# Expert weights of a sandwich kernel: from a resident copy in SBUF to one DRAM load per slot, with the last tiles in slots of their own

## The chip, the cores and the metric

The kernel runs on one core of one Trainium2 chip. The metric is the device time of one execution in microseconds (us); lower is better. The engines are TensorE (PE, with its weight loads as PEld), VectorE (DVE), ScalarE (ACT), GpSimd (POOL) and SyncE (SP), and 16 DMA engines move data.

## What is computed

The input is 16 sequences of 512 tokens with 128 features. Stage one is a state-space block with a convolution and a scan, and a residual. Stage two is a mixture of 16 experts, of which each token uses two:

```python
probs = jax.nn.softmax(xf @ Wr + br, axis=-1)
vals, idx = jax.lax.top_k(probs, K)               # K = 2, E = 16
w = vals / vals.sum(axis=-1, keepdims=True)
...
for ei in range(e):
    h = jax.nn.silu(xf @ W1[ei]) * (xf @ W3[ei])  # 128 -> 512
    y = h @ W2[ei]                                # 512 -> 128
    mu = y.mean(axis=-1, keepdims=True)
    var = ((y - mu) ** 2).mean(axis=-1, keepdims=True)
    y = (y - mu) * jax.lax.rsqrt(var + EPS) * gamma[ei] + beta[ei]
    out = out + combine[:, ei:ei + 1] * y
```

The result gets a layer norm and is added to the tokens that went in.

## The kernel before

Three stages follow one another, all unrolled by Python and put in order by hand, each engine with its own stream.

**Stage one** runs over the 16 sequences (`NS`) as a software pipeline. At its end VectorE picks two experts for each token, ranks the tokens of each expert with a running count (`running`), and GpSimd sends each token's row (128 values, the token's number, its weight; 520 bytes) to its place in the DRAM tensor `slots_scratch` with indirect DMAs (`send_one`, L612). Each expert has a region of its own there.

**Stage two** works through 143 slots (`NSLOT`), a slot being 128 rows of one expert. With 8192 tokens and two experts each there are 16384 rows, and each expert's last tile is not full. So that it holds no stale rows, 128 blank rows are stored behind the end of every region once the counts are known (`store_tail`, L324 to L326; half by SyncE, half by ACT). VectorE works out a table (`slot_table`) with each slot's expert and first row. Four slot columns go through TensorE to one row (the selection matmuls, L2086), and VectorE copies that row (L1536).

For slot j SyncE reads the table and loads the 128 rows to `got`, eight slots ahead (`load_slots`, L490). TensorE transposes them (`x_t`, L2098), ACT copies them to `xsT`. TensorE multiplies by the two up weights (`up`, L2106, 8 passes each for `pA` and `pR`), ACT takes the silu, VectorE multiplies (`hidT`), and TensorE multiplies by the down weights of the slot before (`down`, L2114). VectorE and GpSimd norm and weigh the result (`ers`, `erw`, `yo`), and GpSimd scatters it to `chosen_scratch` (`store`, L698).

The up weights of all 16 experts (8 MB) lie in SBUF in `w13_sb`: SyncE loads four experts (L408, 2 MB) and the other twelve (6 MB) near the end of stage one. ACT copies the 4 KB per partition of the slot's expert to one of four `stage` buffers, two slots ahead (`put_weights`, L1023), from which TensorE reads. The down weights lie in `w2_sb`.

**Stage three** loads both results of each token from `chosen_scratch` to `w13_sb`, adds them on TensorE, norms them and adds `x1`, which lies in `fx1` (one load of 4 MB, L497).

Filler matmuls (`keep_warm`, L1636) stand where TensorE would idle. SyncE's stream is one queue: what stands behind a wait is not issued. The line numbers are those of the kernel before.

## Time and profile before

| | |
|---|---|
| median of 3 runs | 968.43 us (967.34 to 970.10) |
| the profiled execution | 968.34 us, of which 966.5 us are the span |
| granted TensorE clock, mean | 0.99 |
| busy: PE, DVE, ACT, POOL | 97%, 75%, 71%, 64% |
| stage one with the passage to stage two | 0 to 516.6 us |
| expert slots | 516.6 to about 915 us |
| last stage | to 966.5 us |

All times inside the execution are us from the start of its span. A timeline's row gives start, duration, engine, line and operation, output and inputs, count, and in brackets how long the engine was idle before it and what it waited for; "issue" there means that it waited for nothing that the profile shows. A matmul of fp32 shows as two passes. SPq is SyncE's own stream, with the DMAs it issues.

### The profile page before, as it was taken

To read this page: it belongs to the slowest core of one execution; us is meant where nothing else is said; L and a number is where in the kernel's file an instruction comes from. 1 tells how busy PE (TensorE), PEld (TensorE's weight loads), DVE (VectorE), ACT (ScalarE), POOL (GpSimd) and SP (SyncE) were. 2 spreads that over 40 slices of the span, in tenths; PEclk is the share of its full clock that TensorE was granted. 3 is DMA by queue.
4 is the path that set the end of the run, shared out by engine and by line. 5 is a ranking of instruction groups with operands and counts; after the bars stand their busy time and mean duration, and the time that the engine had idled before them with its cause. 6 is when DMAs were issued, how large, how long until landed. Compare 5 with 4: busy or idle time off the path is not lost.

```text
span 966.5 us, 26600 instructions
## 1 busy us (share of the span) xinstructions
PE 933.1 (97%) x7177; PEld 826.0 (85%) x7177; DVE 724.8 (75%) x2524; ACT 688.3 (71%) x1355; POOL 621.8 (64%) x814
## 2 busy tenths in 40 slices
PE   7999999999999999998959999999999999999995
PEld 4777877888878877887949999999999999999962
DVE  2379999999999998898823777677677677777747
ACT  3777787777788787775215778777777777877626
POOL 2445677777777777775661666666666666576647
PEclk9999999999999999999979999999999999999998
DMA  4001322121111111101786211111111111121076
GB/s 137 12 12 34 93 95 84 58 73 54 56 57 50 56 40 42 40 23 42 263 311 192 69 50 49 46 52 51 44 50 50 45 50 47 45 53 49 19 274 248
DMA packets 52255, 75.25 MB, mean 78 GB/s; under 512 B 11103, under 2 KB 30689, under 8 KB 51472
## 3 DMA queue, kind: packets, MB, share of 16 engines
q1 hardware_dynamic: 41632, 54.61, 18.4%
q0 software_dynamic: 8672, 16.93, 5.2%
q10 hardware_dynamic: 1808, 2.02, 0.7%
q8 instruction: 63, 1.03, 0.5%
q14 instruction: 80, 0.66, 0.2%
HBM read 47.09 MB, written 27.41 MB: 77 GB/s over the span
## 4 chain that ended last, share of the span: by engine, by line
PE 79%; DVE 8%; POOL 6%; issue 5%; DMA 1%; ACT 1%; POOLq 0%; DVEq 0%; SPq 0%; ACTq 0%
PE pA L2106 11%; PE pR L2106 11%; PE pA L1665 11%; PE pB L2114 6%; PE pY L2114 5%; PE pY L1779 4%; PE pB L1691 3%; PE pB L1825 3%; PE pA L1680 3%; PE pY L1815 3%; POOL chosen_scratch L698 2%; PE pY L1798 2%; PE pY L1747 2%; PE pA L1636 2%; PE pR L1763 2%
## 5 line engine op out<-in xcount | busy, mean ns | idle before, releaser
L698 POOL DMA_INDIRECT chosen_scratch<-yo,got_id x143 | 148.2, 1036 | 93.7 <-issue 87.9
L1026 ACT ACTIVATE stage<-w_sb 128x1024 f32 x143 | 151.3, 1058 | 56.6 <-issue 56.5
L1545 DVE TENSOR_TENSOR hidT<-pR,sil 128x512 f32<-128x512 f32 x143 | 98.9, 692 | 80.1 <-ACT sil L1021 59.2
L612 POOL DMA_INDIRECT slots_scratch<-xrow,send_at x128 | 134.6, 1052 | 34.1 <-issue 31.2
L2106 PE MATMUL pA<-xsT,stage 128*128 128x128 f32 x1144 | 151.3, 275 | 0.4 <-ACT xsT L1010 0.4
L2106 PE MATMUL pR<-xsT,stage 128*128 128x128 f32 x1144 | 151.1, 275 | 0.0
L2106 PEld LDWEIGHTS pA<-xsT,stage 128*128 128x128 f32 x1144 | 139.2, 192 | 0.7 <-ACT xsT L1010 0.6
L2106 PEld LDWEIGHTS pR<-xsT,stage 128*128 128x128 f32 x1144 | 139.0, 192 | 0.0
L1665 PE MATMUL pA<-xn,taps 128*128 128x512 f32 x256 | 129.8, 593 | 1.0 <-ACT xn L763 1.0
L688 POOL TENSOR_TENSOR ers<-eve,neg_half 128x1 f32<-128x1 f32 x143 | 81.5, 570 | 57.3 <-DVE eve L1557 32.2
L1021 ACT ACTIVATE sil<-pA 128x512 f32<-128x512 f32 x143 | 85.3, 596 | 25.3 <-PE pA L2106 15.3
L564 POOL TENSOR_TENSOR R<-R,dec 128x512 f32<-128x512 f32 x48 | 64.0, 1334 | 40.6 <-ACT Rh L861 40.0
L2114 PE MATMUL pB<-w_sb,hidT 128*128 x576 | 76.2, 275 | 0.0
L2114 PE MATMUL pY<-w_sb,hidT 128*128 x568 | 75.0, 275 | 0.0
L1016 ACT ACTIVATE wb<-gb,got 128x128 f32 x143 | 57.6, 403 | 19.5 <-issue 11.5
L2114 PEld LDWEIGHTS pB<-w_sb,hidT 128*128 128x128 f32 x576 | 70.1, 192 | 0.2 <-issue 0.2
L2114 PEld LDWEIGHTS pY<-w_sb,hidT 128*128 128x128 f32 x568 | 69.1, 192 | 0.0
L1636 PE MATMUL pA<-ident 128*128 128x128 f32 x446 | 57.1, 288 | 0.4 <-issue 0.4
L1636 PEld LDWEIGHTS pA<-ident 128*128 128x128 f32 x446 | 55.3, 204 | 2.0 <-issue 1.8
L1665 PEld LDWEIGHTS pA<-xn,taps 128*128 128x128 f32 x256 | 40.8, 191 | 13.7 <-issue 12.5
L1779 PE MATMUL pY<-G,RT 128*128 128x128 f32 x384 | 50.8, 275 | 0.0
L1570 DVE SCALAR_TENSOR_TENSOR yo<-yg,erw,wb 128x128 f32<-128x128 f32 x143 | 49.1, 343 | 1.6 <-POOL erw L691 1.5
(233 smaller groups left out, 2099.1 us busy)
## 6 DMA issues: line engine op xcount, KB each, us to landing
got<-slots_scratch SPq DMA_DIRECT2D x143, 65.0 KB, 1.8
w_sb<-chosen_scratch SPq DMA_DIRECT2D x16, 512.0 KB, 5.4
w_sb<-in_w_dram SPq DMA_DIRECT2D x1, 6144.0 KB
xin<-in_x_dram SPq DMA_DIRECT2D x16, 256.0 KB
xr<-in_x_dram SPq DMA_DIRECT2D x16, 256.0 KB
x_scratch<-x SPq DMA_DIRECT2D x16, 256.0 KB
w_sb<-in_w_dram SPq DMA_DIRECT2D x4, 1024.0 KB, 8.2
fx<-x_scratch SPq DMA_DIRECT2D x1, 4096.0 KB
```

The lines of the kernel that those rows point to most:

```text
L564: eng.tensor_tensor(halves(R[:, :, :], h)[:, :, 0:h], src, pairs(decs(s, h))[:, :, 1:2].broadcast_to([P, SEQ // h, h]), ALU.mult).then_inc ...
L612: eng.indirect_dma_start(slots_d, bass.IndirectOffsetOnAxis(ap=send_at[:, s % 2, k, t:t + 1], axis=0), xrow[:, s % 2, k, t, :], None).then ...
L688: eng.tensor_tensor(ers[:, q % 2:q % 2 + 1], eve[:, q % 2:q % 2 + 1], neg_half[:, 0:1], ALU.pow).then_inc(epow, 1)
L698: eng.indirect_dma_start(chosen_d, bass.IndirectOffsetOnAxis(ap=got_id[:, j % NGOT:j % NGOT + 1], axis=0), yo[:, q, :], None, bounds_check ...
L1021: eng.activation(sil[:, p, :], pA[:, p, :], ACT.Silu).then_inc(sil_ready, 1)
L1026: eng.activation(stage[:, j % NSTAGE, :, :].rearrange("p k f -> p (k f)"), w13_sb[:, bass.ds(e, 1), :, :].rearrange("p o k f -> p (o k f)" ...
L1545: eng.tensor_tensor(hidT[:, p, :], pR[:, p, :], sil[:, p, :], ALU.mult).then_inc(hid_ready, 1)
L1636: eng.matmul(pA[:, 1, 0:P], w, w, start=True, stop=True)
L1665: i = eng.matmul(pA[:, f, :], taps[:, k, tile(f)], xn[:, s % 2, w], start=k == 0, stop=k == TAPS - 1)
L1779: i = eng.matmul(pY[:, BANK[h], (2 * m + g) * P:(2 * m + g + 1) * P], RT[:, AT[h], g, m, :], G[:, AT[h], g, :], start=True, stop=True)
L2106: i = eng.matmul(out[:, j % 2, tile(c)], stage[:, j % NSTAGE, k, tile(c)], xsT[:, j % 2, :], start=True, stop=True)
L2114: i = eng.matmul((pB, pY)[p][:, 1, 0:D], hidT[:, p, tile(c)], w2_sb[:, c, bass.ds(e, 1), :].rearrange("p o d -> p (o d)"), start=c == 0, s ...
```

## The change

- `w13_sb` is no longer filled with up weights, and ACT's copies are gone. SyncE loads the 512 KB of the slot's expert from DRAM to a `stage` buffer (`load_weights`): it reads the expert from the table, waits until the buffer's last user is through (`h3_mm`), and issues. Each of the four buffers has a semaphore of its own.
- Order on SyncE: `got` of slot 0, weights of slot 0, and so on for four slots, four more `got`; then for each slot the weights (four slots ahead) and, behind a wait for `erw`, `got_id` and `wb` of the slot eight before, the next `got`. The 4 MB of `x1` are loaded in 16 pieces, one at every fourth slot from the 16th to the 76th.
- The table: `running` starts at 128 instead of 0, so rows begin 128 rows into the region. The first 128 rows of every region are blanked at the start (one DMA of 1 MB on SyncE). The full tiles of all experts (a count of (n - 1) // 128 each) take the first 127 slots (`NFULL`). The last 16 slots are one per expert and read the last 128 rows before the expert's end; they may overlap the full tiles or reach into the blank rows. The `store_tail` stores and their semaphores are gone.
- Overlapping rows are stored twice with the same values, and before slot 127's store GpSimd waits until all earlier stores have landed.
- `keep_warm(40)` behind the selection matmuls becomes `keep_warm(22)`. VectorE fills the table's last 16 entries in two further operations. The wait for `gb_loaded` moves to its first use.

```diff
+    NFULL = NSLOT - NE
...
-        def store_tail(eng, e):
-            row = eng.value_load(tail_at[0:1, e:e + 1], min_val=0, max_val=BLANK - P)
-            eng.dma_start(slots_d[bass.ds(row, P), :].rearrange("(p r) d -> p (r d)", r=8), blank[:, :]).then_inc(tails_stored, 16)
...
+            eng.dma_start(slots_d[0:BLANK, :].rearrange("(e r) d -> e r d", e=NE)[:, 0:P, :].rearrange("e (p r) d -> p e (r d)", r=8),
+                          blank[:, :].rearrange("p (o f) -> p o f", o=1).broadcast_to([P // 8, NE, 8 * ROW])).then_inc(blank_stored, 16)
...
-            load_early()
...
-            eng.wait_ge(tail_ready, 1)
-            for e in range(0, NE, 2):
-                store_tail(eng, e)
...
+            def load_weights(j):
+                e = eng.value_load(slot_table[0:1, j:j + 1], min_val=0, max_val=NE - 1)
+                wait_past(eng, h3_mm, j - NSTAGE + 1)
+                eng.dma_start(stage[:, j % NSTAGE, :, :], w13[:, bass.ds(e, 1), :, :].rearrange("p o k f -> p (o k) f")).then_inc(staged[j % NSTAGE], 16)
+
             for j in range(NGOT):
                 load_slots(j)
-            eng.dma_start(fx1[:, :, :, :], x1_d.rearrange("(g p t) d -> p g t d", p=P, t=NT4)).then_inc(fx1_loaded, 16)
-            for n in range(NGOT, NSLOT):
+                if j < NSTAGE:
+                    load_weights(j)
+            for n in range(NGOT, NSLOT + NGOT - NSTAGE):
+                load_weights(n - NGOT + NSTAGE)
+                if n >= NSLOT:
+                    continue
+                if n % 4 == 0 and 4 <= n // 4 < 4 + NG:
+                    g = n // 4 - 4
+                    eng.dma_start(fx1[:, g, :, :], x1_d[g * NT4 * P:(g + 1) * NT4 * P, :].rearrange("(p t) d -> p t d", t=NT4)).then_inc(fx1_loaded, 16)
...
+                if j == NFULL:
+
+                    for k in range(4):
+                        eng.wait_ge(stored[k], len(range(k, NFULL, 4)) * 16)
...
-            put_weights(0)
             xst(0, 0)
-            put_weights(1)
...
-                if j + 2 < NSLOT:
-                    put_weights(j + 2)
...
+                eng.tensor_scalar(running[:, :], running[:, :], float(P), None, ALU.add).then_inc(lower_ready, 1)
...
-            r.step(eng.tensor_scalar(count_i[:, :], count_i[:, :], P - 1, None, ALU.add))
+            r.step(eng.tensor_scalar(count_i[:, :], count_i[:, :], -P - 1, 0, ALU.add, ALU.max))
...
-            eng.tensor_copy(slot_table[:, :], pA[0:1, 0, :]).then_inc(table_ready, 1)
+            r.step(eng.tensor_copy(slot_table[:, :], pA[0:1, 0, :]))
+            eng.tensor_copy(slot_table[0:1, NFULL:NSLOT], iota_es[0:1, :]).then_inc(table_ready, 1)
+            eng.tensor_scalar(slot_table[0:1, TABLE_ROW + NFULL:TABLE_ROW + NSLOT], running[0:1, :], float(-P), None, ALU.add).then_inc(table_ready, 1)
...
-            keep_warm(40)
+            keep_warm(22)
...
-                    eng.wait_ge(staged, j + 1)
+                    eng.wait_ge(staged[j % NSTAGE], j // NSTAGE * 16 + 16)
```

SyncE at the end of stage one, before: the weight loads of 2 and 6 MB, `gamma` and `beta`, then eight tail stores (the last is shown, seven are left out), and the first `got`.

```order
67 L408 DMA w_sb<-in_w_dram 128x12288 [waits y_step]
68 L386 DMA gb<-in_gamma_dram 128x2048
69 L386 DMA gb<-in_beta_dram 128x2048
70 L373 DMA x_scratch<-x 128x512 [waits x1_ready]
...
99 L325 TENSOR_LOAD tail_at
100 L325 ISA x2
101 L326 ISA
102 L326 DMA slots_scratch<-blank 16x1040
103 L492 TENSOR_LOAD slot_table [waits x1_stored,blank_stored,tails_stored,sent0,stage1_dve,sent1,stage1_pool,table_ready,stage1_act,stage1_pe]
104 L492 ISA x2
105 L493 ISA
106 L493 DMA got<-slots_scratch 128x130
```

The same place now. TENSOR_LOAD is the read of the table, the ISA rows belong to it.

```order
67 L373 DMA gb<-in_gamma_dram 128x2048 [waits y_step]
68 L373 DMA gb<-in_beta_dram 128x2048
69 L368 DMA x_scratch<-x 128x512 [waits x1_ready]
70 L457 TENSOR_LOAD slot_table [waits x1_stored,blank_stored,sent0,stage1_dve,sent1,stage1_pool,table_ready,stage1_act,stage1_pe]
71 L457 ISA x2
72 L458 ISA
73 L458 DMA got<-slots_scratch 128x130
74 L461 TENSOR_LOAD slot_table
75 L461 ISA x2
76 L463 ISA
77 L463 DMA stage<-in_w_dram 128x1024
```

The two weight loads and the tail stores are gone, and slot 0's weights stand right behind slot 0's `got`.

SyncE at the start of the loop, before: the x1 load (`fx`), then a `got` load per slot, each behind its wait.

```order
135 L497 DMA fx<-x_scratch 128x16x512
136 L492 TENSOR_LOAD slot_table [waits wb_ready,id_ready,erw_ready]
137 L492 ISA x2
138 L493 ISA
139 L493 DMA got<-slots_scratch 128x130
140 L492 TENSOR_LOAD slot_table [waits wb_ready,id_ready,erw_ready]
141 L492 ISA x2
142 L493 ISA
143 L493 DMA got<-slots_scratch 128x130
```

Now, behind the first eight `got` loads:

```order
118 L461 TENSOR_LOAD slot_table
119 L461 ISA x2
120 L463 ISA [waits h3_mm]
121 L463 DMA stage<-in_w_dram 128x1024
122 L457 TENSOR_LOAD slot_table [waits wb_ready,id_ready,erw_ready]
123 L457 ISA x2
124 L458 ISA
125 L458 DMA got<-slots_scratch 128x130
126 L461 TENSOR_LOAD slot_table
127 L461 ISA x2
128 L463 ISA [waits h3_mm]
129 L463 DMA stage<-in_w_dram 128x1024
```

Each slot has two table reads and two DMAs; the weights of slot 5 stand behind the `got` that waits for `erw` of slot 0.

ACT in one slot of the loop, before:

```order
685 L1021 ACTIVATE sil<-pA 128x512 [waits h1_mm]
686 L1010 ACTIVATE xsT<-pB 128x128 [waits h3_mm,xs_t]
687 L1013 TENSOR_LOAD slot_table
688 L1013 ISA x2
689 L1016 ISA [waits got_loaded1]
690 L1016 ACTIVATE wb<-gb,got 128x128
691 L1024 TENSOR_LOAD slot_table
692 L1024 ISA x2
693 L1026 ISA
694 L1026 ACTIVATE stage<-w_sb 128x1024
```

Now:

```order
647 L999 ACTIVATE sil<-pA 128x512 [waits hid_ready,h1_mm]
648 L986 ACTIVATE xsT<-pB 128x128 [waits h3_mm,xs_t]
649 L989 TENSOR_LOAD slot_table
650 L989 ISA x2
651 L994 ISA [waits got_loaded2]
652 L994 ACTIVATE wb<-gb,got 128x128
```

The table read and the 128 x 1024 copy are gone.

GpSimd's store of slot 127 now, among its neighbours (before, it waited for `yo_ready` and `id_ready` alone):

```order
677 L678 DMA chosen_scratch<-yo,got_id 16384x128 [waits yo_ready,id_ready]
678 L664 TENSOR_TENSOR ers<-eve,neg_half 128x1 [waits evar_ready]
679 L667 TENSOR_TENSOR erw<-ers,got 128x1 [waits yo_ready,epow]
680 L678 DMA chosen_scratch<-yo,got_id 16384x128 [waits stored2,stored1,stored3,stored0,yo_ready,id_ready]
681 L664 TENSOR_TENSOR ers<-eve,neg_half 128x1 [waits evar_ready]
682 L667 TENSOR_TENSOR erw<-ers,got 128x1 [waits yo_ready,epow]
683 L678 DMA chosen_scratch<-yo,got_id 16384x128 [waits yo_ready,id_ready]
```

Behind that store stand the power and `erw` of slot 129.

## Rows read from the trace of the kernel before

The columns of rows 2 are: the stretch and its length, then for PE, PEld, DVE, ACT and POOL the busy us with the number of instructions, the granted clock, the mean busy share of the DMA engines, and GB/s. Rows 10 has the same.

**Rows 1.** shares of the page: busy us, share of the span, instructions

```profile
PE 933.1 (97%) x7177; PEld 826.0 (85%) x7177; DVE 724.8 (75%) x2524; ACT 688.3 (71%) x1355; POOL 621.8 (64%) x814
```

**Rows 2.** table of stretches: busy us per engine, clock, DMA share, GB/s

```profile
499.00:504.60 5.60, 1.49 (x4) 0.53 (x5) 0.00 (x0) 0.00 (x0) 2.95 (x4) 0.54 0.81 215
504.60:509.60 5.00, 4.93 (x24) 4.92 (x24) 0.68 (x1) 0.00 (x0) 0.00 (x0) 0.50 0.54 80
509.60:516.00 6.40, 6.40 (x59) 6.40 (x58) 0.00 (x0) 1.06 (x1) 0.00 (x0) 0.99 0.17 42
530.00:900.00 370.00, 370.00 (x3318) 370.00 (x3318) 260.70 (x930) 294.61 (x531) 238.84 (x399) 1.00 0.19 51
```

**Rows 3.** timeline of TensorE: start us, busy us, what, [idle before]

```profile
489.69 5.66 PE L1636 MATMUL pA<-ident 128*128 128x128 f32 x36
495.33 0.27 PE L2086 MATMUL pA<-ident,slot_cols 128*1 128x128 f32 x1
...
503.92 0.37 PE L2086 MATMUL pA<-ident,slot_cols 128*1 128x128 f32 x1 [1.76 <-issue]
504.67 11.47 PE L1636 MATMUL pA<-ident 128*128 128x128 f32 x80 [0.37 <-issue]
515.98 0.27 PE L2098 MATMUL pB<-ident,got 128*128 128x128 f32 x1
516.62 1.16 PE L2106 MATMUL pA<-xsT,stage 128*128 128x128 f32 x8 [0.37 <-ACT xsT L1010]
...
524.37 1.06 PE L2106 MATMUL pA<-xsT,stage 128*128 128x128 f32 x8
...
527.15 1.06 PE L2106 MATMUL pA<-xsT,stage 128*128 128x128 f32 x8
```

**Rows 4.** groups by line: count, busy us, mean ns, idle before

```profile
L1026 ACT ACTIVATE stage<-w_sb 128x1024 f32 x143 | 151.3, 1058 | 56.6 <-issue 56.5
```

**Rows 5.** timeline of SyncE's DMA issues, 494 to 530

```profile
494.53 13.92 SPq L326 DMA_DIRECT2D slots_scratch<-blank  x7
511.01 8.11 SPq L493 DMA_DIRECT2D got<-slots_scratch  x8
```

**Rows 6.** waits of SyncE, 480 to 530: us in total, times, longest

```profile
SPq L485 <- DMA slots_scratch<-blank: 1.5, 1, 1.5
```

**Rows 7.** timeline of GpSimd, 500 to 525

```profile
501.90 0.96 POOL L612 DMA_INDIRECT slots_scratch<-xrow,send_at  x1 [0.30 <-issue]
```

**Rows 8.** DMA view, 560 to 900: queues, issues, us to landing

```profile
q8 instruction: 28, 0.46, 0.6%
...
got<-slots_scratch SPq DMA_DIRECT2D x122, 65.0 KB, 1.8
chosen_scratch<-yo,got_id POOLq DMA_INDIRECT x122, 2.3
```

**Rows 9.** line L510, the 512 KB loads of the last stage

```profile
L510 SPq DMA_DIRECT2D w_sb<-chosen_scratch x16: 359/360/471, 923.4 to 943.0; - x16
...
DMA to landing us min/median/max: 3.8/5.4/7.4
```

**Rows 10.** table of stretches, in the 2 MB weight load

```profile
464.00:468.00 4.00, 3.28 (x29) 2.90 (x27) 3.86 (x7) 2.88 (x6) 3.08 (x4) 1.00 1.03 383
```

**Rows 11.** timeline of VectorE, 495 to 525

```profile
505.03 0.68 DVE L1536 CAST slot_table<-pA 1x512 int32<-1x512 f32 x1 [10.05 <-PE pA L2086]
```

**Rows 12.** timeline of one slot in the loop, 699.5 to 706

```profile
699.98 3.13 SPq L493 DMA_DIRECT2D got<-slots_scratch  x2
...
700.08 1.06 PE L2106 MATMUL pA<-xsT,stage 128*128 128x128 f32 x8
...
701.83 0.19 POOL L691 TENSOR_TENSOR erw<-ers,got 128x1 f32<-128x1 f32 x1
```

**Rows 13.** DMA view, 516 to 530: issues with median us to landing

```profile
chosen_scratch<-yo,got_id POOLq DMA_INDIRECT x2, 5.6
```

**Rows 14.** chain of waits at the loop's end

```profile
921.20 2.11 DMA chosen_scratch<-yo,got_id
```

More of the change, by code:

```diff
@@ L101, in sandwich @@
     chosen_d = nc.dram_tensor("chosen_scratch", [2 * NTOKENS, D], fp32).ap()
-    assert NSLOT <= 2 * P and BLANK + P < NOWHERE
+    assert NSLOT <= 2 * P and NFULL >= (2 * NTOKENS - 1) // P and BLANK + P < NOWHERE
     ctx = ExitStack()
@@ L322, in sandwich @@
         sum_bank = lambda g: w13_sb[:, 0, 0, :] if g == 0 else (pA, pB, pR, pY)[g % 8 // 2][:, g % 2, :]
-        def store_tail(eng, e):
-            row = eng.value_load(tail_at[0:1, e:e + 1], min_val=0, max_val=BLANK - P)
-            eng.dma_start(slots_d[bass.ds(row, P), :].rearrange("(p r) d -> p (r d)", r=8), blank[:, :]).then_inc(tails_stored, 16)
         blank_ready, blank_stored, e_loaded = sem("blank_ready"), sem("blank_stored"), sem("e_loaded")
         pool_passed, dve_passed = sem("pool_passed"), sem("dve_passed")
-        w13_loaded = sem("w13_loaded")
-        staged = sem("staged")
+        staged = [sem(f"staged{q}") for q in range(NSTAGE)]
         w2_loaded = sem("w2_loaded")
@@ L339, in sandwich @@
         stage1_sp = sem("stage1_sp")
-        tables, tail_ready, tails_stored = sem("tables"), sem("tail_ready"), sem("tails_stored")
+        tables = sem("tables")
         cols_ready, cols_mm, table_ready = sem("cols_ready"), sem("cols_mm"), sem("table_ready")
@@ L482, in _ @@
                 eng.wait_ge(q, 1)
-            eng.wait_ge(tails_stored, 16 * NE)
-            eng.wait_ge(blank_stored, 16)
+            eng.wait_ge(blank_stored, 32)
             for p in range(2):
                 eng.wait_ge(sent[p], NS // 2 * 2 * NT4 * 16)
-            eng.wait_ge(table_ready, 1)
+            eng.wait_ge(table_ready, 2)
             def load_slots(j):
@@ L997, in _ @@
             eng.nop().then_inc(stage1_act, 1)
-            eng.wait_ge(tail_ready, 1)
-            for e in range(1, NE, 2):
-                store_tail(eng, e)
             for q in (stage1_pe, stage1_dve, stage1_pool, stage1_sp):
                 eng.wait_ge(q, 1)
-            eng.wait_ge(gb_loaded, 32)
-            eng.wait_ge(table_ready, 1)
+            eng.wait_ge(table_ready, 2)
             def xst(j, p):
@@ L1013, in weighed_beta @@
                 e = eng.value_load(slot_table[0:1, j:j + 1], min_val=0, max_val=NE - 1)
+                if not j:
+                    eng.wait_ge(gb_loaded, 32)
                 wait_past(eng, yo_ready, j - 3)
@@ L1021, in silu @@
                 eng.activation(sil[:, p, :], pA[:, p, :], ACT.Silu).then_inc(sil_ready, 1)
-            def put_weights(j):
-                e = eng.value_load(slot_table[0:1, j:j + 1], min_val=0, max_val=NE - 1)
-                wait_past(eng, h3_mm, j - NSTAGE + 1)
-                eng.activation(stage[:, j % NSTAGE, :, :].rearrange("p k f -> p (k f)"), w13_sb[:, bass.ds(e, 1), :, :].rearrange("p o k f -> p (o k f)"), ACT.Copy).then_inc(staged, 1)
-            eng.wait_ge(w13_loaded, 32)
-            put_weights(0)
             xst(0, 0)
-            put_weights(1)
             for j in range(NSLOT):
@@ L1550, in normalise @@
                 e = eng.value_load(slot_table[0:1, j:j + 1], min_val=0, max_val=NE - 1)
+                if not j:
+                    eng.wait_ge(gb_loaded, 32)
                 eng.wait_ge(yo_mm, j + 1)
```

36 lines of the change are left out of this document (4 added, 32 removed).

## The prediction

> **What bounds the kernel now.** I read three views in this order. First the page's shares: TensorE is busy for 97% of the span [rows 1]. That figure hides two things, the filler matmuls (L1636) and the clock, so next comes the table of stretches. From 530 to 900 us, the expert loop, TensorE is busy for the whole 370 us at full clock, with the DMA engines at 0.19 [rows 2]. One slot takes 2.79 us there (527.15 less 524.37 at the start of the loop, [rows 3]). Nothing but TensorE sets the pace, and ACT, which copies the weights of every slot (143 copies of 1058 ns, 151.3 us, [rows 4]), only fills its own idle time. **Taking the copies off ACT is therefore worth nothing in the loop by itself.** The time can move in the passage between the stages. The last real work of stage one on TensorE ends near 489.7, the first matmul of an expert starts at 516.62 [rows 3], and the chain of waits between them is filler, eight gaps of "issue" and 80 more filler passes. The eight selection passes of L2086 take 9 us (495.33 to 504.3) where their own time is 0.27 to 0.37 each, and the filler behind them runs to 515.98 [rows 3]. In the same stretch SyncE stores seven blank tails for 13.92 us, waits 1.5 us for them to land, and issues the first load of `got` only at 511.01 [rows 5, 6].
>
> **The change, part by part.**
>
> *Tails.* The sixteen stores of `blank` at known row counts go, and with them the wait for `tails_stored`. What is late next for SyncE is the end of the sends. GpSimd issues the last one at 501.90 [rows 7]; a store of the same kind lands 2.3 us after its issue [rows 8], so at 504.2. From the wait for the tails (508.45 + 1.5 = 509.95, and about 0.1 more) to the first `got` issue at 511.01 were 0.96 us. With 0.3 us for the semaphores between GpSimd and SyncE (an estimate) the first `got` is issued at 504.2 + 0.3 + 0.96 = 505.5, where it was 511.01.
>
> *First weights.* They no longer lie in SBUF. SyncE issues `got` and weights in turn, and one such issue with its table read costs (8.11 - 0.34)/7 = 1.11 us [rows 5]. Slot 0's weights go out at 506.6. The trace has no load of 512 KB of 4 KB pieces, so I bound its landing. Below stands the `got` load, 65 KB in 1.8 us [rows 8]; above stands the 512 KB load of the last stage, 5.4 us in the median with a least of 3.8, several of them queued behind one another [rows 9]. The fixed part of the first plus the data at the rate that the DMA engines show at full share (524 KB at 383 GB/s, 1.4 us, [rows 10]) is 3.2 us. I take that, since in the loop the DMA engines are at 0.19 and the load queues behind nothing. Slot 0 can start at 509.8.
>
> *Filler and clock.* `keep_warm` goes from 40 to 22 calls, 80 to 44 passes. If the selection passes lose their gaps (the 6 MB weight load, the tail stores and the table reads of SyncE and ACT that ran beside them are gone) the filler is over near 502 (44 passes at 6.40/59 = 0.108 us, [rows 2]), and TensorE idles for some 7 us. In the trace TensorE was sparse from 495.3, the clock stood at half (0.54) from 499, and it was full again only at 509.6, 5.0 us after the filler had resumed [rows 2]. The same after 509.8 costs 2.5 us. Slot 4 starts 10.53 us after slot 0 [rows 3], so at 509.8 + 10.5 + 2.5 = 522.8, where it was 527.15: **4.3 us gained**. If the gaps stay, the selection ends at 504.3, the filler at 511.8 (24 passes in the 5.0 us at half clock, 20 at 0.108), the table is copied by 505.71 [rows 11], two small DVE operations of some 0.2 us follow, and with the 0.96 of above the first `got` goes out near 507.1. Slot 4's weights are the thirteenth issue: 507.1 + 12 x 1.11 = 520.4, and land at 523.6: 3.5 us gained. In the first case the thirteenth issue lands at 518.8 + 3.2 = 522.0, just in time. I take 4.2.
>
> *The loop.* Each slot now adds a table read and a 512 KB load on SyncE. The load for slot j+5 stands behind the `got` load that waits for `erw` of slot j. From the steady part [rows 12]: slot j+2 starts at 700.08, `erw` of slot j starts at 701.83, and the `got` issue follows 0.94 later (699.98 is behind the `erw` one slot of 2.79 us earlier, 699.04). The weights go out 1.11 later, at 703.88, which is 3.80 after slot j+2 began. Slot j+5 starts 3 x 2.79 = 8.37 after it. **The load has 4.57 us to land**, against the 3.2 taken. SyncE itself works 2 x 1.11 us of 2.79, and 0.43 us more in the 16 slots that carry a piece of the x1 load. The DMA engines get 1.4 us of 2.79 on top of 0.19, in all 0.69. One instruction packet holds an engine for about 1.2 us (28 packets, 0.6% of 16 engines over 340 us, [rows 8]): 3.2 + 1.2 = 4.4 is still inside, but with little left, and where two such things meet TensorE waits a few tenths. I put **0.5 us** on the loop (an estimate; bounds 0 and the rival below).
>
> *Last tiles in slots of their own.* The number of slots stays 143. At slot 127 GpSimd waits until all earlier stores have landed. Behind the waiting store stand the power and `erw` of slot 129, and behind these SyncE. The store before it went out 2.79 us earlier and lands after 2.3 [rows 8], so the wait is over when it is reached; with the 5.6 us of the busiest stretch [rows 13] it would be 2.8 us once. The blank slots now lie inside the first 127, so the very last store is a real one: it lands in 2.3 instead of 2.11 us [rows 14], **0.2 us lost**.
>
> *At nothing.* The blank store of 1 MB at the start (SyncE, covered by stage one, where TensorE runs without it), one DVE operation on 16 columns, the x1 load in 16 pieces (it was one 4 MB load beside slots that kept their pace), `gb_loaded` waited for later.
>
> Sum against the profiled execution: 968.34 - 4.2 + 0.2 + 0.5 = 964.8. The median of the runs is 0.09 above it, which gives **964.9**.
>
> **The rivals.**
>
> *The weights come late in the loop.* The point from which it decides is a mean landing of 4.57 us. Every 0.1 us beyond it lengthens a cycle of five slots by 0.1, so the loop by 0.1 x 139/5 = 2.8 us. At 4.9 us, between 4.4 and the 5.4 of the last stage, 0.33 gives 9.2 us: 964.4 + 9.2 = 974. At 5.4 it would be 987. For it: the least 512 KB load took 3.8, not 3.2, and the margin is one instruction packet. Against it: the 5.4 belongs to a queue of such loads, and here each is alone.
>
> *The passage gives nothing.* The stall ends later than I think and the clock stays low longer. With 5.4 us for the first weights slot 0 starts at 512.0; with the clock at half for 10 us, as in the trace from 499 to 509.6, it loses 5 us: slot 4 at 527.5, no gain, 969. Against it: both have to go wrong together.
>
> *The pitch of the rows in DRAM.* Each partition's 4 KB lie 64 KB apart. If reads at that pitch ran at half rate, a slot's load would hold the DMA engines for 2.7 us, and with 0.19 x 2.79 = 0.5 they would need 3.2 us a slot: 0.4 x 143 = 59 us more, 1022. The row speaks against it: the 2 MB load of four experts at the same pitch ran at 383 GB/s [rows 10], though in pieces of 16 KB. The Trainium skill ("DMA: Bandwidth & Descriptors", "Latency and other measured facts") says that row pitches at large powers of two in HBM cost rate, and lists a large loss from 2 MiB on and next to none at 512 KiB. By its figures this pitch would be harmless, and the trace agrees as far as it goes.
>
> *It does better.* Without loss of clock and with 1.8 us of landing, slot 4 would start when its weights are there, 518.8 + 1.8 = 520.6: 6.5 us gained, 962.
>
> **How the numbers follow.** The forecast case gets 0.60 (964.9, its own range 962.0 to 966.5), late weights 0.20, the empty passage 0.15, the pitch 0.05. A measurement of this kernel can tell about 0.3%, 2.9 us: faster is below 965.5. Faster gets 0.54 (0.06 of the forecast case lies nearer), the same 0.22 (0.06, 0.12 of the empty passage, 0.04 of weights that are only a little late), slower 0.24 (0.16, 0.03, 0.05). The range goes from the best case, 962.0, to 975.0; outside it lie the pitch, the heavy half of the late weights, and 0.04 below.
>
> **What would show it.** In the profile of the changed kernel: the first `got` near 505.5, the first weights in `stage` some 4.3 us behind it, selection passes without gaps, the first expert matmul near 510 at half clock, slot 4 near 523; in the loop TensorE full at 2.79 us a slot, landings near 3.2 us, DMA near 0.7, no wait of L2106's up matmuls for a load. Wrong would be landings over 4.5 us, waits of TensorE for `stage` in the loop, GpSimd standing at slot 127 for more than 1 us, or an expert loop that is not full.

## The result, and the profile after

| | before | after |
|---|---|---|
| median | 968.01 us (967.34 to 970.10, 4 runs) | 975.37 us (974.31 to 975.98, 4 runs) |
| ratio | | 1.0066, interval 1.0045 to 1.0087 |
| span of the profiled execution | 966.5 us | 974.1 us |
| granted TensorE clock, mean | 0.99 | 0.991 |

The forecast was 964.9 us with a range from 962.0 to 975.0. The change makes the kernel slower by 0.66%, where the forecast had it 0.4% faster. The page of after, shares and queues:

```profile
PE 934.8 (96%) x7141; PEld 824.9 (85%) x7141; DVE 724.4 (74%) x2526; ACT 538.1 (55%) x1212; POOL 621.2 (64%) x814
...
q1 hardware_dynamic: 62192, 121.74, 42.3%
...
q8 instruction: 63, 1.03, 0.5%
...
HBM read 113.67 MB, written 27.41 MB: 145 GB/s over the span
```

TensorE's busy time is that of [rows 1], plus 1.7 us, in a span that is 7.6 us longer. It is kept from work, and not slowed in it. SyncE's queue (q1) fills 42% of the 16 DMA engines (18.4% before): 143 loads of 0.52 MB stand in the place of 8.4 MB, most of the 113.67 MB read. q8 is the 63 instruction packets of 16 KB that are spoken of below; a further 80 instruction packets of 8 KB go over q14. TensorE's timeline shows the passage between the stages (start us, busy us, what, idle before and its releaser):

```profile
494.38 1.03 PE L2055 MATMUL pA<-ident,slot_cols 128*1 128x128 f32 x8
496.42 0.73 PE L1605 MATMUL pA<-ident 128*128 128x128 f32 x5 [1.01 <-issue]
...
502.15 4.86 PE L1605 MATMUL pA<-ident 128*128 128x128 f32 x26 [0.42 <-issue]
...
510.66 1.13 PE L2075 MATMUL pA<-xsT,stage 128*128 128x128 f32 x8 [2.73 <-DMA stage<-in_w_dram]
...
513.09 1.13 PE L2075 MATMUL pA<-xsT,stage 128*128 128x128 f32 x8 [0.29 <-DMA stage<-in_w_dram]
...
522.76 1.13 PE L2075 MATMUL pA<-xsT,stage 128*128 128x128 f32 x8 [1.07 <-issue]
```

and SyncE's first issues stand there so:

```profile
505.70 0.36 SPq L458 DMA_DIRECT2D got<-slots_scratch  x1
506.85 0.35 SPq L463 DMA_DIRECT2D stage<-in_w_dram  x1
```

This half went as forecast. The first `got` goes out at 505.70 (forecast 505.5, before 511.01 [rows 5]), slot 0 starts at 510.66 (509.8, before 516.62 [rows 3]), slot 4 at 522.76 (522.8, before 527.15 [rows 3]). Slot 4 is **4.4 us earlier** than before. The table of stretches, as [rows 2], has the other half in its last line:

```profile
499.00:504.60 5.60, 4.68 (x18) 4.03 (x19) 0.90 (x3) 0.00 (x0) 2.40 (x3) 0.50 0.11 36
504.60:509.60 5.00, 2.71 (x19) 2.36 (x18) 0.02 (x1) 0.28 (x1) 0.00 (x0) 0.93 0.38 98
509.60:516.00 6.40, 5.04 (x43) 4.91 (x44) 1.36 (x2) 2.33 (x6) 0.00 (x0) 1.00 0.88 240
530.00:900.00 370.00, 362.83 (x3215) 359.86 (x3214) 252.22 (x898) 150.21 (x387) 230.78 (x387) 1.00 0.80 240
```

From 530 to 900 us TensorE is busy for 362.83 us where it was busy for all 370 [rows 2], at full clock. The waits from 530 to 925 us (total us, times, longest) say where it stood:

```profile
PEld pA L2075 <- issue: 10.1, 17, 1.7
...
PE pA L2075 <- issue: 6.9, 10, 1.6
```

These are the first up matmuls of a slot, whose last input is the `stage` buffer. "issue" as the releaser means only that the profile found none. The prediction had the landing time of a weight load at 3.2 us. The profile of a second execution of the changed kernel gives it so (least, median, most):

```profile
DMA to landing us min/median/max: 3.5/3.8/5.5
```

The span splits at five points that every profile of this study has, each in us: the last send of stage one (when it is issued), from it to the first issue for slot 0, from there to slot 0's first up matmul, slot 0 to slot 4, slot 4 to slot 142, and from there to the end.

| profile | last send | to first issue | to slot 0 | 0 to 4 | 4 to 142 | to the end |
|---|---|---|---|---|---|---|
| before | 501.90 | 9.11 | 5.61 | 10.54 | 384.90 | 54.44 |
| before, again | 502.93 | 7.46 | 2.76 | 12.44 | 384.90 | 54.70 |
| after | 501.05 | 4.65 | 4.96 | 12.10 | 397.15 | 54.19 |
| after, again | 502.23 | 3.56 | 4.94 | 12.29 | 394.21 | 53.87 |
| after, third | 503.69 | 4.90 | 5.05 | 12.01 | 397.12 | 54.13 |
| weights alone | 502.69 | 4.98 | 4.89 | 12.84 | 389.90 | 54.80 |
| weights alone, again | 505.55 | 6.49 | 5.08 | 12.29 | 392.30 | 54.99 |
| tails alone | 502.21 | 3.57 | 2.74 | 11.85 | 384.90 | 54.23 |
| tails alone, 42 fillers | 502.43 | 3.59 | 2.65 | 10.55 | 384.90 | 54.78 |
| weights a slot earlier | 503.74 | 3.55 | 4.96 | 12.28 | 384.90 | 53.86 |
| weights a slot later | 500.78 | 3.59 | 5.04 | 13.84 | 487.40 | 54.94 |
| half loads | 500.84 | 3.59 | 4.04 | 12.11 | 385.81 | 54.81 |
| weights before rows | 504.52 | 4.86 | 4.95 | 13.29 | 386.41 | 53.97 |
| fill 31 | 502.44 | 4.83 | 5.76 | 11.17 | 396.32 | 54.08 |
| fill 40 | 503.76 | 4.85 | 6.95 | 10.48 | 399.00 | 55.26 |
| earlier and first | 500.82 | 4.81 | 6.79 | 10.48 | 384.90 | 54.99 |

From before to after: stage one ended 0.85 us sooner in this execution, the passage up to slot 4 is 25.26 - 21.71 = 3.55 us shorter, the loop **12.25 us longer**, the end 0.25 shorter. Together 7.6 us, the difference of the spans. The column of the loop is the finding. It is 384.90 us, to the hundredth, in every kernel in which TensorE never waits (138 slots of 2.789 us). What exceeds that is stalls.

Single stalls can be read. The longest in the loop is that of slot 120. GpSimd, SyncE and TensorE of after, in this order:

```profile
844.77 1.03 POOL L678 DMA_INDIRECT chosen_scratch<-yo,got_id  x1 [0.94 <-issue]
...
849.99 1.03 POOL L678 DMA_INDIRECT chosen_scratch<-yo,got_id  x1 [3.30 <-DVE yo L1539]
...
851.72 0.19 POOL L667 TENSOR_TENSOR erw<-ers,got 128x1 f32<-128x1 f32 x1
```

```profile
848.53 0.34 SPq L463 DMA_DIRECT2D stage<-in_w_dram  x1
...
853.85 0.24 SPq L463 DMA_DIRECT2D stage<-in_w_dram  x1
```

```profile
857.56 1.13 PE L2075 MATMUL pA<-xsT,stage 128*128 128x128 f32 x8 [1.56 <-issue]
```

The two stores of GpSimd start 5.22 us apart, where 2.79 is usual, so `erw` comes at 851.72 and SyncE, which waits for it, issues the rows late and the weights behind them at 853.85, 5.3 us after the issue before. They land in the usual time and TensorE has stood 1.56 us. The profile puts GpSimd's wait down to a `yo` of VectorE, but that is a later one. The `yo` of this store is

```profile
845.99 0.34 DVE L1539 SCALAR_TENSOR_TENSOR yo<-yg,erw,wb 128x128 f32<-128x128 f32 x1
```

so its input had been there for 3.7 us. The pause is in the kernel before too, at the same store, and no row there shows TensorE waiting:

```profile
839.63 1.03 POOL L698 DMA_INDIRECT chosen_scratch<-yo,got_id  x1 [0.94 <-issue]
...
844.85 1.03 POOL L698 DMA_INDIRECT chosen_scratch<-yo,got_id  x1 [3.30 <-DVE yo L1570]
```

### The profile page after: what moved, and what is told of

Same layout as the page of the kernel before. It is cut to its first block, busy times and chain, and to the rows that moved or that the text cites. A ratio compares the mean times of both kernels' runs of the same rounds, so it can differ in the third digit from the quotient of the medians.

```text
span 974.1 us, 26589 instructions
## 1 busy us (share of the span) xinstructions
PE 934.8 (96%) x7141; PEld 824.9 (85%) x7141; DVE 724.4 (74%) x2526; ACT 538.1 (55%) x1212; POOL 621.2 (64%) x814
## 3 DMA queue, kind: packets, MB, share of 16 engines
q8 instruction: 63, 1.03, 0.5%
HBM read 113.67 MB, written 27.41 MB: 145 GB/s over the span
## 4 chain that ended last, share of the span: by engine, by line
PE 85%; DVE 8%; issue 3%; POOL 1%; DMA 1%; another core or an unknown queue 1%; ACT 1%; SPq 0%; DVEq 0%; ACTq 0%; POOLq 0%
PE pA L2075 14%; PE pR L2075 13%; PE pA L1634 11%; PE pB L2083 7%; PE pY L2083 7%; PE pY L1748 4%; PE pB L1660 3%; PE pB L1794 3%; PE pA L1649 3%; PE pY L1784 2%; PE pY L1767 2%; PE pY L1716 2%; PE pR L1732 2%; PE pA L1605 2%; PE pB L2067 2%
## 5 line engine op out<-in xcount | busy, mean ns | idle before, releaser
L1605 PE MATMUL pA<-ident 128*128 128x128 f32 x410 | 54.5, 289 | 2.8 <-issue 2.7
L1605 PEld LDWEIGHTS pA<-ident 128*128 128x128 f32 x410 | 51.3, 203 | 4.4 <-issue 4.4
L540 POOL TENSOR_TENSOR R<-u,dec 128x512 f32<-128x512 f32 x16 | 24.2, 1510 | 40.0 <-ACT dec L790 40.0
```

What stands on the lines that cost most here:

```text
L540: eng.tensor_tensor(halves(R[:, :, :], h)[:, :, 0:h], src, pairs(decs(s, h))[:, :, 1:2].broadcast_to([P, SEQ // h, h]), ALU.mult).then_inc ...
L1605: eng.matmul(pA[:, 1, 0:P], w, w, start=True, stop=True)
```

## The experiments

Each edit is to the changed kernel if not said otherwise, and each ratio is to the kernel before.

**Is it the margin?** The weights were issued one slot earlier, ahead of the wait for `erw`:

```diff
+            load_weights(NSTAGE)
             for n in range(NGOT, NSLOT + NGOT - NSTAGE):
-                load_weights(n - NGOT + NSTAGE)
+                if n - NGOT + NSTAGE + 1 < NSLOT:
+                    load_weights(n - NGOT + NSTAGE + 1)
```

> The changed kernel, with the weights of each slot issued one slot earlier in SyncE's stream: ahead of the wait for erw that they stood behind. Bytes, buffers and the number of DMAs stay. Theory (margin): a load is issued 4.57 us before its slot, lands some 3.9 us after its issue, and every disturbance over 0.7 us stalls TensorE; with a slot more, about 7.3 us, the loop is full at 2.79 us a slot. Of the 14.0 us that the loop lost, the 1.2 at slot 4 stay (the thirteenth issue): 975.4 - 12.8 = 962.6 (961.5 to 964). Rival (the DMA engines at 0.8 are themselves the limit, or reads of DRAM slow down the rest): the same bytes in the same time, so 975, within 1.

Measured: 965.26 us, 0.9979 (0.9964 to 0.9994), span 963.3. The stretch from 530 to 900:

```profile
530.00:900.00 370.00, 370.00 (x3319) 370.00 (x3318) 260.42 (x931) 154.68 (x398) 238.91 (x398) 1.00 0.83 249
```

TensorE stands nowhere, though the DMA engines are as full as in after (0.83 against 0.80). The loads land no sooner (the median to the last packet is 3.4 us in both). Between issue and use are now 7.4 us instead of 4.5. The loop's whole loss is gone. The time is 2.7 us above the expectation; in the profiled execution stage one ended 2.7 us later than in after's (503.74 against 501.05).

Then one slot later:

```diff
-                if j < NSTAGE:
+                if j < NSTAGE - 1:
                     load_weights(j)
-            for n in range(NGOT, NSLOT + NGOT - NSTAGE):
-                load_weights(n - NGOT + NSTAGE)
+            for n in range(NGOT, NSLOT + NGOT - NSTAGE + 1):
+                load_weights(n - NGOT + NSTAGE - 1)
```

> The changed kernel with the weights issued one slot later in SyncE's stream. Bytes and DMAs stay. Margin theory, with the margin 2.79 us shorter (1.8 us): every slot waits. The weights of slot j+4 are issued 6.6 us after slot j+1 begins (down of slot j, its statistics, erw, the got issue, 1.1) and land 3.9 later, so three slots take 10.5 us, 3.5 each, and the run takes 972 + 0.71 x 139 = 1071 (1055 to 1085). Rival (the DMA engines' throughput is the limit): no change, 970 to 976.

Measured: 1067.23 us in one run, span 1065.6. Waits from 530 to 925, and the landing of the loads:

```profile
PEld pA L2075 <- issue: 75.9, 100, 1.7
...
PE pA L2075 <- issue: 58.6, 85, 1.5
```

```profile
DMA to landing us min/median/max: 3.5/3.7/5.2
```

The waits are now on nearly every slot, and the loop takes 102.5 us more. The landing is 3.7 us in the median, as good as unchanged. It is the distance from issue to use that decides, not the traffic.

And in between: SyncE issues the weights before the rows, 1.11 us earlier.

```diff
+                load_weights(n - NGOT + NSTAGE + 1)
                 load_slots(n)
```

> The changed kernel with one thing swapped: behind the wait for `erw` SyncE issues the weights first and the rows second, so a weight load is issued 1.11 us earlier and has 4.57 + 1.11 = 5.68 us; the rows come 1.11 us later, where they have several slots to spare. Theory (the tail of the landing times against the margin): the stalls of the changed kernel are 0.1 to 1.3 us each but for slot 120 (1.7), so nearly all vanish and slot 120 keeps 0.6: slot 4 to slot 142 in 385.0 to 386.5 us (385 without a stall, 394 to 399 in the changed kernel), ratio to the kernel before 0.996 to 0.999. Rival (it is not the margin but SyncE's own queue or the rows that come late): above 390 us, ratio over 1.001.

Measured: 967.36 us, 0.9976 (0.9965 to 0.9987), span 968.0. From 530 to 900:

```profile
530.00:900.00 370.00, 368.97 (x3306) 368.64 (x3305) 259.61 (x925) 154.26 (x397) 236.49 (x396) 1.00 0.86 247
```

The loop takes 386.41 us, inside the expectation. So 1.1 us of margin removes 8 to 11 of 9 to 12 us. Over the four places of the issue the loop's loss is 102.5 us (one slot later), 9.3 to 12.25 (as changed, three profiles), 1.5 (1.11 us earlier) and 0 (one slot earlier).

**Is it the size of the load?** Only W1's half is loaded, 256 KB; W3 is left out of the computation.

```diff
-                eng.dma_start(stage[:, j % NSTAGE, :, :], w13[:, bass.ds(e, 1), :, :].rearrange("p o k f -> p (o k) f"))
+                eng.dma_start(stage[:, j % NSTAGE, 0:1, :], w13[:, bass.ds(e, 1), 0:1, :].rearrange("p o k f -> p (o k) f"))
```

> The changed kernel, but each slot loads only the first up weight (256 KB), and both up matmuls use it, so W3 is left out of the result. Order and number of DMAs stay. Margin theory: 0.65 us less of data brings the landing from 3.9 to 3.2 us, so that a disturbance of 1 us no longer shows; what remains is the late issues (slot 4, GpSimd's own pauses): 965 (963 to 968). Rival (the issues come late, since SyncE or GpSimd are late, and the size is nothing): 974 to 975.

Measured: 964.72 us, 0.9977 (0.9961 to 0.9994), span 961.2. The landing:

```profile
DMA to landing us min/median/max: 2.6/2.8/4.0
```

Half the bytes save 1.0 us (3.8 to 2.8). Of the loop's loss 0.91 us is left, 0.76 of it at slot 120. Halving the load and issuing it earlier do the same thing for the loop, as the margin theory says.

**Which half of the change does what?** The kernel before with the DRAM loads alone (old tails and table, `keep_warm(40)`, sixteen `x1` pieces):

```diff
-                eng.activation(stage[:, j % NSTAGE, :, :].rearrange("p k f -> p (k f)"), w13_sb[:, bass.ds(e, 1), :, :].rearrange("p o k f -> p (o k f)"), ACT.Copy).then_inc(staged, 1)
...
+                eng.dma_start(stage[:, j % NSTAGE, :, :], w13[:, bass.ds(e, 1), :, :].rearrange("p o k f -> p (o k) f")).then_inc(staged[j % NSTAGE], 16)
```

> The kernel before, with only the weights part of the change: the DRAM loads per slot on SyncE and the x1 load in pieces; tails, their stores, the old slot table and 40 filler calls as before. Margin theory: the loop loses the same 13 to 14 us and the passage gains nothing (first got at 511.0, slot 0's weights 1.1 + 3.9 behind it, slot 0 at 516 to 516.6): 968.4 + 14 = 982 (979 to 984). Rival (the loss comes from the slots' new order, the wait at slot 127 or the doubled stores): about 968.

Measured: 974.45 us, 1.0072 (1.0047 to 1.0097), span 970.1. It is slower by 7.6 us and not by the 14 that I expected. In the profiled execution (971.87 us, the fastest of the six) its loop lost 5.0 us. The other half, the new tails, table and `keep_warm(22)` with the resident weights:

```diff
-                load_weights(n - NGOT + NSTAGE)
...
+                load_w13(4, NE)
...
+                if j + 2 < NSLOT:
+                    put_weights(j + 2)
```

> The changed kernel with the resident weights and ACT's copies of before put back: only the tails' slots, the table, 22 filler calls and the x1 load in pieces stay. First got at 505.7, slot 0's weights need no load behind it, so slot 0 starts near 508.4 instead of 516.6 and the loop is full: 968.4 - 8.2 + 0.2 = 960.4 (959.5 to 963). Rival (the passage's gain came from the missing 8 MB load, whose traffic slows the sends and the sequencers): slot 0 near 514 to 516, 966 to 968.

Measured: 961.93 us, **0.9941** (0.9921 to 0.9961), span 959.5. The tails are the gain and the weights the loss. The two do not simply add: 0.59% gained and 0.72% lost would make 0.13%, and the whole change lost 0.5 to 0.7%. The passage of the kernel with the tails alone, on TensorE:

```profile
507.70 0.45 PE L2082 MATMUL pB<-ident,got 128*128 128x128 f32 x1 [5.18 <-DMA got<-slots_scratch]
508.52 2.08 PE L2090 MATMUL pA<-xsT,stage 128*128 128x128 f32 x8 [0.37 <-ACT xsT L991]
...
512.00 1.06 PE L2090 MATMUL pA<-xsT,stage 128*128 128x128 f32 x8
```

Slot 0 starts 2.74 us behind the first `got`, not 4.96. But it runs at half clock (2.08 us for eight up passes that take 1.06), behind 5.18 us of idling. So with 42 instead of 22 filler calls:

```diff
-            keep_warm(22)
+            keep_warm(42)
```

> The tails part alone (resident weights, ACT's copies), with 42 filler calls instead of 22 behind the selection matmuls. In the profile of the tails alone the filler ended at 502.5, TensorE idled 5.2 us and slot 0 ran at half clock (3.5 us from its first pass to slot 1's, instead of 2.1). With filler up to some 507 the clock stays full and slot 0 starts no later: 1.4 us less than the tails alone, 0.9925 of before. Rival (the filler runs past the first got where the passes are slow, and delays slot 0): no gain or 1 us lost, 0.994 to 0.995.

Measured: 961.21 us, 0.9941 (0.9928 to 0.9954), span 958.9. The profile shows the effect of the filler,

```profile
508.00 0.30 PE L2082 MATMUL pB<-ident,got 128*128 128x128 f32 x1 [1.58 <-DMA got<-slots_scratch]
508.67 1.16 PE L2090 MATMUL pA<-xsT,stage 128*128 128x128 f32 x8 [0.37 <-ACT xsT L991]
...
510.74 1.16 PE L2090 MATMUL pA<-xsT,stage 128*128 128x128 f32 x8
```

so slots 0 to 4 take 10.55 instead of 11.85 us, but the ratio to the kernel before has not moved. This is the rival's number.

**Do the kernels repeat?** Both were run once more.

> The kernel before once more, for its profile beside those of this series: every theory expects the times of before. The selection passes of L2086 either spread over 9 us again (a property of the kernel) or run in 1 us, as they did in the four experiments so far (a property of the execution).

> The changed kernel once more, in the series of the experiments. Margin theory: some 0.7% over before again (973 where before is 967), and the stalls of TensorE in the loop sit on slots whose load landed more than 4.1 us after its issue or was issued late. If the weights alone cost only what they did in the experiment on them (+0.7%), then the tails of the change bring little beside them: 969 to 974.

Measured: 967.01 us for before, 1.0001 (0.9987 to 1.0014), and 972.76 for after, 1.0053 (1.0034 to 1.0072). The profile of before showed something that I had taken for a property of the kernel:

```profile
496.30 1.03 PE L2086 MATMUL pA<-ident,slot_cols 128*1 128x128 f32 x8
497.27 9.20 PE L1636 MATMUL pA<-ident 128*128 128x128 f32 x80
512.34 0.44 PE L2098 MATMUL pB<-ident,got 128*128 128x128 f32 x1 [5.88 <-DMA got<-slots_scratch]
513.15 2.07 PE L2106 MATMUL pA<-xsT,stage 128*128 128x128 f32 x8 [0.37 <-ACT xsT L1010]
```

The eight selection passes take 1.03 us with no gap, not 9 us with eight gaps [rows 3], in the same kernel.

**What makes single loads late?** In the trace each 16 KB instruction packet holds a DMA engine for 0.9 to 2.1 us. Over nine profiles of kernels that load 512 KB per slot I took each load's time from issue to last packet, by the moment at which an instruction packet started beside it:

| instruction packet starts, us behind the issue | loads | median to last packet | over 4.1 us |
|---|---|---|---|
| none | 948 | 3.41 | 6% |
| 0 to 0.55 | 63 | 3.44 | 3% |
| 0.55 to 0.95 | 100 | 3.81 | 29% |
| 0.95 to 3.0 | 111 | 4.36 | 66% |
| over 3.0 | 11 | 3.29 | 0% |

The smaller instruction packets, of 8 KB, have no effect of this size: among the loads without a 16 KB packet those that have one of 8 KB beside them take 3.43 us in the median, the others 3.39, with 6% over 4.1 us in both groups.

TensorE starts 0.45 us behind the last packet, so with 4.54 us from issue to use 4.1 is the limit. In the first two profiles of the changed kernel the packets start 0.95 and 1.0 us behind the issue in the median, in that of the weights alone 0.35. That would explain why the weights alone lose less. To move the packets I gave TensorE more instructions ahead of the loop, beside a third run of the changed kernel:

```diff
-            keep_warm(22)
+            keep_warm(31)
```

> The changed kernel as it is, once more, beside the next two. Two profiles of it gave 397.15 and 394.21 us from slot 4 to slot 142, where the kernel before takes 384.90, while the variant with the weights alone changed lost only 5.0. In the two profiles most instruction packets start 0.8 to 1.5 us after the issue of a weight load, in the weights-alone variant 0.1 to 0.5. Theory (the moment of the instruction packets decides how much is lost, and it belongs to the kernel): packets again 0.8 to 1.5 us behind the issue, slot 4 to slot 142 in 393.5 to 397.5 us, ratio 1.004 to 1.008. Rival (it is luck of each execution): the moment of the packets elsewhere, the loop anywhere from 389 to 397.

> The changed kernel with 31 instead of 22 filler calls behind the selection matmuls: 36 more instructions on TensorE (18 passes of 0.11 us, in time in which it waits for the first rows), so that TensorE's instruction packets (16 KB each) begin elsewhere in its stream. Nothing else differs. Theory: the loss of the loop follows the moment at which the instruction packets start, counted from the issue of the weight load beside them. If most start within 0.6 us of an issue, slot 4 to slot 142 takes 389 to 391.5 us; if most start 1.0 to 2.0 us behind it, 394 to 399. Rival: the loop loses what r2_after loses, within 2 us, wherever the packets start.

> The same with 40 filler calls, as many as in the kernel before: 72 more instructions than the changed kernel. Theory: as for 31 calls, the loss of slots 4 to 142 follows the moment of the packets: 389 to 391.5 us if most start within 0.6 us of an issue, 394 to 399 if most start 1.0 to 2.0 us behind it. Rival: within 2 us of r2_after. In the passage: the filler then ends near 506.5 instead of 502.4, TensorE idles some 1.2 and 2.6 us, the clock stays full or nearly, and slot 0 to slot 1 takes 2.1 to 2.4 us instead of 3.8; but slot 4 waits for the thirteenth issue either way, so less than 0.4 us of this reaches the time.

Measured: 974.86 us and 1.0051 (1.0031 to 1.0071) for the changed kernel, 974.78 and 1.0049 (1.0025 to 1.0073) with 31 calls, 976.39 and 1.0060 (1.0035 to 1.0084) with 40. The loops took 397.12, 396.32 and 399.00 us, in profiled executions of 978.57, 976.25 and 981.97 us, all above their medians. The packets came in other slots (6, 10, 15, 19 with 31 calls and 6, 10, 14, 18 with 40, instead of 7, 11, 15, 20, so they follow TensorE's instructions), but their moment stayed, 1.0, 0.9 and 1.0 us behind the issue in the median. So the edit didn't move what it was to move, and can't tell the theory from its rival. The weights alone, again:

> The variant with the weights alone changed (old tails), a second execution. If its small loss belongs to the kernel: instruction packets again 0.1 to 0.6 us behind the issues, 388.5 to 391.5 us from slot 4 to slot 142. If it belongs to the execution: 394 us or more. I hold the first likelier, 0.65, since three profiles of the changed kernel agreed on where the packets lie.

Measured: 978.55 us in one run, loop 392.30, packets 0.6 us behind the issue in the median with half of them in the first 0.6. The place of the packets came back roughly. The loss, 7.4 us, lies between both expectations, and only 1.1 us of it is on loads with a packet beside them.

The stalls of the loop, split by whether a 16 KB instruction packet starts between the issue and the landing of the load, show where the two kernels differ (us):

| profile | on loads with a packet | on the others |
|---|---|---|
| after | 7.2 | 5.0 |
| after, again | 5.3 | 4.0 |
| after, third | 8.2 | 4.0 |
| weights alone | 0.6 | 4.4 |
| weights alone, again | 1.1 | 6.3 |

The loads without a packet cost about the same in both. What the whole change loses beyond the weights alone is on the loads with one. This is a count over five profiles and no experiment that moved the packets.

**What is the best that the DRAM loads give?** One slot earlier, weights ahead of the rows for slots 0 to 3, those of slot 4 as tenth issue, 42 fillers:

```diff
             for j in range(NGOT):
-                load_slots(j)
                 if j < NSTAGE:
                     load_weights(j)
+                load_slots(j)
+                if j == NSTAGE:
+                    load_weights(j)
```

> The version with the weights one slot earlier, and three more edits in the passage: weights of slot 0 to 3 ahead of the rows of the same slot, weights of slot 4 right behind the rows of slot 4 (the tenth issue instead of the thirteenth), 42 filler calls. Expected against the version with the weights one slot earlier (ratio 0.9979): slot 0 starts 1.1 us sooner after the first issue (weights are its last input, 3.9 us behind their issue), slots 0 to 4 take 10.6 us instead of 12.3, no stall in the loop (384.90 from slot 4 to slot 142): 2.8 us less, ratio 0.995 (0.9935 to 0.9965). Rival: the clock or the issues of SyncE hold slots 1 to 4 as before, and only 1.1 us or less is won: ratio 0.997 or above. The best version so far keeps the weights in SBUF and has only the new tails (0.994).

Measured: 966.58 us, 0.9974 (0.9962 to 0.9987), span 962.8. This is the rival's number. On TensorE,

```profile
502.02 9.84 PE L1608 MATMUL pA<-ident 128*128 128x128 f32 x70 [0.62 <-issue]
...
512.42 1.16 PE L2078 MATMUL pA<-xsT,stage 128*128 128x128 f32 x8 [0.45 <-ACT xsT L989]
```

the filler had gaps here and ended only at 511.9. Slot 0 waited for it, not for its weights. More filler keeps the clock, and costs the same again whenever its issue is slow. The best version measured is the one with the tails alone. Even where the DRAM loads cause no stall in the loop they cost time ahead of it: from the last send to slot 4 are 20.79 us with the weights one slot earlier and 18.16 with the tails alone.

## Why the prediction was wrong

Term by term, the forecast had 4.2 us gained in the passage, 0.5 lost in the loop and 0.2 lost at the end. The profiled execution has 4.4 gained up to slot 4, 12.25 lost in the loop and 0.25 gained at the end. The loop is the term that failed.

**The passage: right in size, partly by luck.** From the last send to the first issue the prediction put 3.6 us (505.5 less 501.90). With the new tails it is 3.55 to 3.59 in six profiles, and 4.65 to 4.90 in the six in which TensorE's instructions had gaps in that stretch. There SyncE waits last for the table, which VectorE writes late too: in after the selection passes end at 495.41, and the copy starts at 503.67; in the second profile it starts at 497.33, 0.04 us behind them. After is one of the profiles with gaps, and met 505.5 only because its stage one ended 0.85 us sooner. The weights of slot 0 were used 3.8 us behind their issue, not 3.2. The clock was at half from 499 to 504.6 (0.50) and full again by slot 0, so the 2.5 us put on it did not come in after. In the second profile slot 0 did run at half clock, and still slots 0 to 4 took only 12.29 us against 12.10. In both, slot 4 waited for its weights, the thirteenth issue, as in the prediction's second case. The errors cancelled: 4.4 us, of which 3.55 are the change's.

**The filler and the gaps: half right.** In after the eight selection passes did lose their gaps (494.38, 1.03 us). But the gaps did not go with the 6 MB load and the tail stores: the filler behind the passes has them up to 502.15, at a spacing of some 1.4 us, and the kernel before has an execution without any. It is a property of the execution. The filler ended at 507.0 and not near 502. Compared like with like, the passage up to slot 4 gives 3.55 us with gaps and 1.87 without (22.66 to 20.79), not 4.2.

**The loop: here it failed.** The margin was worked out right: 4.57 us forecast, 4.54 measured. **The mis-sized term is the landing: 3.8 us in the median (least 3.5) where the prediction took 3.2.** That left 0.7 us of slack and not 1.4, and the loop lost 12.25 us (9.3 in the second profile) where 0.5 was put. With half the bytes and a landing of 2.8 us the loss is 0.9. The prediction chose the fixed part of a 65 KB load plus bytes at the full rate. But the bounds it named held a better row, the least of the 512 KB loads, 3.8 us [rows 9]. It was set aside as a queued one, and the measured landing of the new loads is just that. The Trainium skill ("DMA: Bandwidth & Descriptors", "Anatomy of one DMA") has for one DMA of the GpSimd path 2.0 us plus the bytes at 436 GB/s, for 512 KB an estimate of 3.2 us as well. The loads here go out from SyncE, in 4 KB pieces, and the measurement, which decides, is 0.6 above that.

**The instruction packet: right mechanism, wrong sum.** The prediction put 3.2 + 1.2 = 4.4 "still inside" 4.57. With 3.8 it is 5.0, outside. In after, eight stalls over 0.6 us lie behind slot 4, six of them on loads with such a packet beside them, and all stalls on such loads sum to 7.2 us. The Trainium skill ("Runtime: NRT & Kernel Launch", "Instruction fetch mechanics") says that engines fetch in 16 KiB blocks and that the cost of a block is mostly hidden. For the engine that fetches the trace agrees: the loops without stalls take 384.90 us with 32 or 33 such packets in them. For a data load with under a microsecond to spare it is not so.

**The rival.** "The weights come late" had 0.20 and a point of decision at a mean landing of 4.57. Its time, 974, is near what came, but by luck: it stood for a mean landing of 4.9 us, and the landing measured is 3.8 in the median, below its point. Each late load costs its own excess once, plus about 0.07 us in the next slot, and does not lengthen a cycle of five. What decides is the share of loads beyond the margin and not the mean. So the sum of 0.5 us for the loop should have been made over the spread (most 5.5 against 4.57), not with one typical load.

**Slot 127** was put at nothing, or at 2.8 us once. GpSimd's gap there, ahead of the second row, is

```profile
885.31 1.03 POOL L678 DMA_INDIRECT chosen_scratch<-yo,got_id  x1 [0.63 <-issue]
...
889.18 1.03 POOL L678 DMA_INDIRECT chosen_scratch<-yo,got_id  x1 [1.71 <-issue]
```

1.71 instead of the usual 0.63 us, 1.1 us more. It makes the weights of slot 134 late: 0.4 us of stall in after, 0.95 in the second profile and 0.02 in the third. **The GpSimd pause** was in the trace before and is in no term of the sum. It costs 1.6 to 1.95 us at slot 120 in the three profiles of the changed kernel and the two of the weights alone. **The x1 pieces** were put at nothing as well. The weights of every fourth slot from 13 to 73 stand behind one, and these 16 of 138 slots carry 1.1 to 3.2 us of the loop's loss in the changed kernel and 1.8 and 2.8 us in the weights alone. No run takes the pieces away. The DMA share of the loop was 0.80 where 0.7 was forecast, and is not the limit: at 0.83, with the weights one slot earlier, nothing stalled. The pitch of the rows in DRAM did no harm, as forecast: a 4 KB piece held its DMA engine for 159 ns in the median, which is 412 GB/s on 16 of them. The 0.2 us for the last store do not show: from slot 142 to the end are 53.87 to 54.19 us with the change, and 54.44 and 54.70 before.

**What stays open.** The weights alone lose 5.0 and 7.4 us in the loop, the whole change 9.3 to 12.25. The barrier at slot 127 accounts for 0.02 to 0.95 us of this, by the stall at slot 134. The rest of the difference sits on loads with an instruction packet beside them. Why these packets start 0.9 to 1.1 us behind the issue in the changed kernel and 0.35 to 0.6 in the other is not known, and no run moved them. So that the packets make the difference is argued from the traces and not shown by an edit. Without the barrier overlapping rows would be stored unordered, so that wasn't tried.

## What to carry to other kernels

A transfer that replaces a resident copy needs a margin that covers the spread of its landing and not only its median. Here the median was 3.8 us, the most 5.5, the margin 4.57, and 0.7 us of slack cost 12 us in 138 slots, while issuing the weights 1.1 us earlier cost nothing and gave almost all back. Take the landing from the nearest row of the same size and shape, even where its conditions look worse, and list what else the issuing queue waits behind (here GpSimd, through `erw`), since its hiccups are free only as long as nobody waits. When two edits come together, measure them apart: the tails alone gave 0.6%, the weights alone took 0.7%.

## What the runs showed of the hardware

- A 512 KB load from DRAM in 4 KB pieces lands in 3.5, 3.8 and 5.5 us (least, median, most), one of 256 KB in 2.6, 2.8 and 4.0 by the view above. The DMA engines are busy for 0.80 of the loop in the one case and 0.57 in the other.
- Loads beside which a 16 KB instruction packet starts 1 to 3 us behind the issue land 0.95 us later in the median (4.36 against 3.41 us). Where it starts in the first half microsecond they don't (3.44).
- GpSimd starts the store of slot 113 5.22 us behind the one before it (5.32 in one profile) instead of 2.79, in all sixteen profiles of twelve kernels, with the store's inputs ready. It is the one behind 844.77 in after and 839.63 in before. The cause is open.
- In some executions of one and the same kernel TensorE's instructions between the stages come with gaps of 0.2 to 2 us, at a spacing of 0.7 or 1.4 us, and in others without. The copy of the table on VectorE is late in the same executions. Two profiles of the kernel before differ so, and their passages by 2.6 us (25.26 against 22.66). The cause is open.
